# Another order of the projections, stacks and router stages within the step of an attention kernel

## The reference

```python
def attention(h, mask, ctx, Wq, Wk, Wv, Wo, gate):          # 32 heads of 16
    q, k, v = heads(h @ Wq), heads(h @ Wk), heads(h @ Wv)
    q, k = q * cos + rotate_half(q) * sin, k * cos + rotate_half(k) * sin
    own = softmax(q @ k.T / 4 + mask) @ v
    ak, av = heads(ctx @ Wk), heads(ctx @ Wv)
    return (own + tanh(gate) * softmax(q @ ak.T / 4) @ av) @ Wo

x = x + attention(layernorm(x), mask, ctx, Wq, Wk, Wv, Wo, gate)
h = layernorm(x)
value, expert = top_k(h @ router_w.T, 2)                     # of 8 experts
weight = softmax(value)
x = x + sum over the two of weight * (silu(h @ w1[expert].gate) * (h @ w1[expert].up)) @ w2[expert]
```

## Time and profile before

| | |
|---|---|
| time, median of 3 runs | 2524.99 us (2516.36 to 2528.28) |
| profiled execution | 2524.06 us |
| its span | 2522.1 us |
| TensorE, VectorE, ScalarE, GpSimd busy | 82%, 57%, 50%, 33% of the span |
| TensorE clock granted, mean | 0.914 of full speed |
| attention phase | up to about 1,950 us of the span |

### The profile page before, as it was taken

The page is one execution under the profiler, slowest core; times in us unless marked ns, Lnnn a source line. Parts: engine busy times, 40 slices in busy tenths (PEclk is TensorE's granted clock), DMA queues, the critical chain, the costliest instruction groups (busy, mean ns, idle before and its releaser), DMA issues. The chain is left out here.

```text
span 2522.1 us, 55300 instructions
## 1 busy us (share of the span) xinstructions
PE 2069.4 (82%) x18953; PEld 1234.9 (49%) x18954; DVE 1444.9 (57%) x3715; ACT 1258.6 (50%) x2260; POOL 821.0 (33%) x851
## 2 busy tenths in 40 slices
PE   4888888888788877878788888888888449999997
PEld 2455555544444444544444444544445226666664
DVE  4567666666666666666666666666666433333332
ACT  4565555555555555555455555555555234444443
POOL 2123323233233222232223232222222334444443
PEclk7899989899889888998898989899999769999999
DMA  2001111000000000010000000000001234444444
GB/s 101 21 29 32 30 35 47 29 29 29 29 29 29 29 29 29 29 29 29 29 29 29 29 29 29 29 29 29 29 25 20 52 85 83 84 83 84 83 84 66
DMA packets 69810, 105.95 MB, mean 42 GB/s; under 512 B 25024, under 2 KB 29120, under 8 KB 69120
## 3 DMA queue, kind: packets, MB, share of 16 engines
q0 software_dynamic: 24096, 37.51, 8.6%
q1 hardware_dynamic: 45536, 65.69, 8.4%
HBM read 67.51 MB, written 35.65 MB: 41 GB/s over the span
## 5 line engine op out<-in xcount | busy, mean ns | idle before, releaser
L515 ACT ACTIVATE pr<-st 128x512 f32<-128x512 f32 x512 | 305.0, 596 | 451.0 <-PE st L1083 335.1
L1051 PE MATMUL md<-kk,qz 128*128 128x128 f16 x2048 | 221.1, 248 | 203.1 <-DVE mx L714 79.9
L379 POOL TENSOR_TENSOR t<-t 128x512 f32<-128x512 f32 x64 | 81.4, 1271 | 872.1 <-DVE t L692 872.1
L710 DVE TENSOR_REDUCE mx<-md 128x4 f32<-128x512 f32 x256 | 176.5, 689 | 299.0 <-remote 218.9
L1097 PE MATMUL av<-pr,vv 128*17 128x128 f32 x4096 | 253.6, 293 | 66.4 <-issue 56.1
L1051 PEld LDWEIGHTS md<-kk,qz 128*128 128x128 f16 x2048 | 136.1, 108 | 314.3 <-issue 169.4
L1431 PE MATMUL y<-w1s,hgT 128*128 x1704 | 280.3, 315 | 4.6 <-ACT hgT L1345 4.6
L414 POOL DMA_INDIRECT lists<-row,posi x256 | 248.8, 972 | 86.4 <-issue 86.4
L1074 PE MATMUL st<-qz,kk 128*128 128x256 f16 x1024 | 204.9, 283 | 41.8 <-DVE mT L735 37.1
L507 ACT ACTIVATE qz<-ma 64x256 f16<-64x256 f16 x512 | 191.8, 375 | 79.8 <-remote 65.8
L1431 PEld LDWEIGHTS y<-w1s,hgT 128*128 128x128 f16 x1704 | 164.5, 98 | 96.6 <-issue 5.1
(11 more groups left out here) (200 smaller groups left out, 3875.0 us busy)
## 6 DMA issues: line engine op xcount, KB each, us to landing
wst<-in_w SPq DMA_DIRECT2D x32, 352.0 KB, 3.1
cin<-in_ctx SPq DMA_DIRECT2D x32, 256.0 KB, 4.1
xin<-in_x SPq DMA_DIRECT2D x32, 256.0 KB, 3.8
xres<-in_x SPq DMA_DIRECT2D x32, 256.0 KB, 3.8
out<-x SPq DMA_DIRECT2D x32, 256.0 KB, 2.1
h_pairs<-ohs SPq DMA_DIRECT2D x32, 256.0 KB
lists<-row,posi POOLq DMA_INDIRECT x256
msk<-in_mask SPq DMA_DIRECT2D x32, 64.0 KB, 3.6
```

The lines of the kernel that those rows point to most:

```text
L515: act.activation(pr[:, path, :, :], st[path][:, :, :], ACT.Exp).then_inc(p_ex.sem, 1)
L710: dve.tensor_reduce(mx[:, 1, 4 * g:4 * g + 4], sm[1][:, :, :], AX.X, ALU.max).then_inc(s_ad.sem, 1)
L1051: i = pe.matmul(sm[path][:, j, :], qz[:, h // 2, h % 2, :], keys[:, h // 2, :], start=True, stop=True)
```

## The change

TensorE's step: the query and key projections of the batch after the next now stand at the end (`q(m)` after scores 7, `k(m)` after the last turn back), so that the next step finds them done. The value projections stand between the stacks (`v` with u = 11, `avp` with u = 13) and use `ma[1]` both. Context turn, output turn, output projection, h turn and router come one or two half-groups sooner, stack 0 with u = 7 and scores 0 with u = 8. Tables at the top of the file give the places of stacks and scores and their banks. ScalarE follows. On VectorE the fourth `normal` of a batch moves from the end of its step to the start of the next, and `router_weights` and `router_rows` move from the first third of the step to behind maxima 4. GpSimd's and SyncE's lists are unchanged. `first` and `last` are adapted.

```diff
+STACK_AT = (7, 8, 9, 10, 11, 12, 14, 15)
+SCORES_AT = (8, 9, 10, 11, 12, 13, 15)
+STACK_BANK = (0, 1, 0, 1, 0, 0, 0, 1)
...
@@ scalar: own_values, stack_out
-            act.activation(vv[:, n.par, 0, :, 0:HD], heads(ma[0]), ACT.Copy, scale=1 / WS).then_inc(v_v.sem, 1)
+            act.activation(vv[:, n.par, 0, :, 0:HD], heads(ma[1]), ACT.Copy, scale=1 / WS).then_inc(v_v.sem, 1)
-            bank, pairs = half(ma[g % 2]), slice(2 * g, 2 * g + 2)
+            bank, pairs = half(ma[STACK_BANK[g]]), slice(2 * g, 2 * g + 2)
@@ scalar: step
                 exps(b, u)
-                if u == 0:
+                if u == 0 and n:
+                    ctx_hi(n)
+                    mask_hi(n)
+                if u == 1:
+                    if n:
+                        q_high(n)
                     if d:
                         out_hi(d)
+                if u == 2 and n:
+                    ctx_turned(n)
+                if u == 3 and d:
+                    out_T(d)
+                if u == 4:
                     if n:
-                        ctx_hi(n)
-                        mask_hi(n)
-                if u == 2:
-                    if n:
-                        q_high(n)
+                        k_high(n)
                     if c:
                         router_exp(c)
-                if u == 3:
-                    if d:
-                        out_T(d)
-                    if n:
-                        ctx_turned(n)
-                if u == 4 and n:
-                    k_high(n)
                 if u >= 5 and u % 4 == 1:
                     values_T(b, u // 4 - 1)
-                if u == 5:
-                    w_slice(b)
+                if u == 5 and n:
+                    ak_high(n)
                 if u == 6:
                     if d:
                         h_high(d)
-                    if n:
-                        ak_high(n)
-                if u == 8 and d:
+                    w_slice(b)
+                if u == 7 and d:
                     h_transposed(d)
                 if u == 11 and m:
                     x_high(m)
-                if u >= 8 and n:
-                    stack_out(n, u - 8)
-            values_T(b, 3)
-            if n:
-                own_values(n)
-                adapter_values(n)
+                if u == 12 and n:
+                    own_values(n)
+                if u == 14 and n:
+                    adapter_values(n)
+                if n and u in STACK_AT:
+                    stack_out(n, STACK_AT.index(u))
             if m:
                 x_turned(m)
+            values_T(b, 3)
@@ vector: neg_max, step
-            if b:
-                normal(b, 3)
             dve.wait_ge(mp_t.sem, mp_t.at(n))
             dve.tensor_copy(mT[:, :, :], m_bank()[0:3 * NH]).then_inc(m_T.sem, 1)
...
+            if n:
+                rotate_q(n)
             if d:
-                out_low(d)
+                normal(d, 3)
             if n:
                 ctx_lo(n)
                 mask_lo(n)
-                rotate_q(n)
+            if d:
+                out_low(d)
             if c:
                 router_top(c)
             if n:
                 rotate_k(n)
-            if c:
-                router_weights(c)
             if d:
                 residual(d)
                 norm_h(d, n)
-            if c:
-                router_counts(c)
-                router_rows(c)
-            if d:
                 h_low(d)
             if n:
                 ak_low(n)
+            if c:
+                router_counts(c)
             normal(b, 0)
...
             if n:
                 maxima(n, 1)
+                maxima(n, 2)
             normal(b, 1)
             if n:
-                for g in range(2, 5):
-                    maxima(n, g)
+                maxima(n, 3)
+                maxima(n, 4)
+            if c:
+                router_weights(c)
+                router_rows(c)
+            if n:
+                maxima(n, 5)
             normal(b, 2)
             if n:
-                for g in range(5, 8):
-                    maxima(n, g)
-                neg_max(n, b)
-            else:
-                normal(b, 3)
+                maxima(n, 6)
+                maxima(n, 7)
+                neg_max(n)
@@ tensor: waits of x_turn, k, v, avp, stack
-            pe.wait_ge(v_v.sem, v_v.at(n.shift(-1)))
+            pe.wait_ge(stk_o.sem, stk_o.at(n.shift(-1), GROUPS - 1))
...
-            pe.wait_ge(av_v.sem, av_v.at(n.shift(-1)))
+            pe.wait_ge(x_T.sem, x_T.at(n))
+            pe.wait_ge(stk_o.sem, stk_o.at(n.shift(-1)))
...
-            pe.wait_ge(stk_o.sem, stk_o.at(n, GROUPS - 1))
-            project(ma[0], xT, wv).then_inc(v_p.sem, 1)
+            pe.wait_ge(stk_o.sem, stk_o.at(n, 4))
+            project(ma[1], xT, wv).then_inc(v_p.sem, 1)
...
-            pe.wait_ge(stk_o.sem, stk_o.at(n))
+            pe.wait_ge(v_v.sem, v_v.at(n))
...
-            if g >= 2:
+            if g in (2, 3, 4):
                 pe.wait_ge(stk_o.sem, stk_o.at(n, g - 1))
+            if g in (5, 6):
+                pe.wait_ge(stk_o.sem, stk_o.at(n, g))
+            if g == 7:
+                pe.wait_ge(av_v.sem, av_v.at(n))
@@ tensor: step
                 if u >= 6 and u % 4 == 2:
                     values_back(b, u // 4 - 1)
+                if u == 4 and n:
+                    ak(n)
+                if u == 7 and d:
                     router(d)
+                if n and u in STACK_AT:
+                    stack(n, STACK_AT.index(u))
+                if n and u in SCORES_AT:
+                    scores(n, SCORES_AT.index(u))
                 if u:
                     values(b, u - 1)
+                if u == 1 and n:
+                    ctx_turn(n)
+                if u == 2 and d:
+                    out_turn(d)
+                if u == 3 and d:
+                    out_project(d)
                 if u == 5 and c:
                     places(c, n)
+                if u == 6 and d:
+                    h_turn(d)
+                if u == 11 and n:
+                    v(n)
+                if u == 13 and n:
+                    avp(n)
+            if m:
+                x_turn(m)
             values(b, 2 * GROUPS - 1)
             if n:
                 scores(n, GROUPS - 1)
-                v(n)
-                avp(n)
+            if m:
+                q(m)
+            if n:
+                max_turn(n)
             values_back(b, 3)
             if m:
-                x_turn(m)
-            if n:
-                max_turn(n)
+                k(m)
```

More of the change, by code:

```diff
@@ L606, in first @@
             for g in range(GROUPS):
+                if g == 5:
+                    own_values(n)
+                if g == 6:
+                    adapter_values(n)
                 stack_out(n, g)
-            own_values(n)
-            adapter_values(n)
             x_turned(n.shift(1))
@@ L714, in maxima, with neg_max @@
             dve.tensor_reduce(mx[:, 0, 4 * g:4 * g + 4], sm[0][:, :, :], AX.X, ALU.max).then_inc(s_own.sem, 1)
-        def neg_max(n, b=None):
+        def neg_max(n):
             dve.wait_ge(s_own.sem, s_own.at(n))
@@ L911, in last @@
         def last(n):
+            normal(n, 3)
             router_top(n.shift(-1))
@@ L1035, in stack @@
                 pe.wait_ge(f_cnt.sem, f_cnt.at(n.shift(-3)))
-            if g >= 2:
+            if g in (2, 3, 4):
                 pe.wait_ge(stk_o.sem, stk_o.at(n, g - 1))
-            turn_pairs(qs, ma[g % 2], 0, 2 * g, 2)
-            turn_pairs(ks, ma[g % 2], 2, 2 * g, 2)
-            turn_pairs(aks, ma[g % 2], 4, 2 * g, 2).then_inc(stk_t.sem, 1)
+            if g in (5, 6):
+                pe.wait_ge(stk_o.sem, stk_o.at(n, g))
+            if g == 7:
+                pe.wait_ge(av_v.sem, av_v.at(n))
+            bank = ma[STACK_BANK[g]]
+            turn_pairs(qs, bank, 0, 2 * g, 2)
+            turn_pairs(ks, bank, 2, 2 * g, 2)
+            turn_pairs(aks, bank, 4, 2 * g, 2).then_inc(stk_t.sem, 1)
         def scores(n, g):
@@ L1139, in step @@
                     values_back(b, u // 4 - 1)
-                if u == 9 and d:
+                if u == 4 and n:
+                    ak(n)
+                if u == 7 and d:
                     router(d)
-                if u >= 9 and n:
-                    stack(n, u - 8)
-                if u == 1 and n:
-                    q(n)
-                if u == 2 and n:
-                    k(n)
-                if u == 4 and d:
-                    out_project(d)
-                if u == 5 and n:
-                    ak(n)
+                if n and u in STACK_AT:
+                    stack(n, STACK_AT.index(u))
+                if n and u in SCORES_AT:
+                    scores(n, SCORES_AT.index(u))
                 if u:
                     values(b, u - 1)
-                if u == 3:
-                    if n:
-                        ctx_turn(n)
-                    if d:
-                        out_turn(d)
+                if u == 1 and n:
```

(19 more changed lines are left out.)

## The result

| | before | after |
|---|---|---|
| time, median (lowest to highest, 4 runs each) | 2526.64 us (2516.36 to 2531.44) | 2728.63 us (2726.52 to 2733.82) |
| profiled execution, its span | 2524.06, 2522.1 us | 2733.82, 2731.8 us |
| TensorE clock granted, mean | 0.914 | 0.883 |

The changed kernel is slower: ratio 1.081 (95% interval 1.077 to 1.085). The prediction had the sign and missed the size: 2585 was forecast, its range ended at 2655.

The account below looks back on a forecast made before the run. TensorE (82% busy) bounds front and tail, VectorE paces the middle, list DMAs lose 6.3 us. Step 56.6 + 0.4 branch + 5.0 lists + 1.0 irregular = 63.0 against 61.1; 28 steps plus 8 us give about 2585 us, range 2440 to 2655.

Parts of the forecast that it names:

- The order without lists: Whole step free of the list loss: 56.6 us against 52.2 now, plus 0.4 for the loop's backward branch.
- The lists: End of step: eight list DMAs move to x = 45.5 to 55.4, their loss onto the chain, 5.0 us (0 to 7.9).
- irregular: Whole step: 1.0 us for the pauses that already make some steps 62 to 68 us.
- Tail and front: Step's end and start: 5.2 us of projections leave the front, yet stack 0 comes at x = 25.0, now 24.0.
- high outputs to 7.2, their rests to 8.0: Front, ScalarE then VectorE: high outputs done at x = 7.2, their rests at 8.0, output projection from 10.9 to 13.5.
- the 5.2 us that left the front turn into waits of TensorE; the front gives back nothing: Front, TensorE: 5.2 us of moved projections become waits, no gain; bounds for the front minus 2 to plus 2.
- Middle: Maxima 0 at x = 27.9 to maxima 7 ending at 54.9: VectorE waits behind value projections, router operations add 2.5 us.
- rival B: Whole step: VectorE's waits close and the norm's chain comes earlier, 3 us a step less than forecast, 2495 us; chance 0.18.
- the 62.9 for a loss that stays at x = 40: Step time in us if, by the skill page's sentence, the list loss stays at x = 40 at its present cost.
- rival C: End of step: the whole list loss lies on the chain, 7.9 us instead of 5.0, total 2665 us; chance 0.15.
- The branch: Loop end: the backward branch costs 0.4 us a step, 0.8 in each second step.
- Rival A: End of step: the list loss falls off the chain behind projections needing few semaphores, step 58, total 2445 us; chance 0.22.

Follow-up runs that it names:

- outputs first: Changed kernel with high outputs ahead of high queries on ScalarE: 2669.80 us, ratio 1.046 to the kernel before.
- both cures: Changed kernel with high outputs ahead of high queries on ScalarE, and four filler matmuls before each wait of output projection, h turn and router: 2613.22 us, ratio 1.024.
- late rows: Kernel before with only router weights and rows moved behind maxima 4, so list DMAs start later: 2473.98 us, ratio 0.976.

## Why the prediction was right in sign and wrong in size

Forecast 63.0 us a step, measured 68.3; the 5.3 split as follows. The order without lists: predicted 57.0 with the branch, measured 61.0, so 4.0. The lists: predicted 5.0 plus 1.0 irregular, measured 7.4, so 1.4. The 4.0 in turn are 5.3 for lock and clock, which the sum did not have, less 1.3 that it counted too much elsewhere.

*Tail and front.* First scores at x = 2.8 (predicted 2.7), the turn's wait in the list-free step 0.73 (0.8): right. The step that failed is "high outputs to 7.2, their rests to 8.0". I gave the rests their lone duration and had read the neighbour only from the other side: the earlier trace rows show what GpSimd's rests do to a small VectorE operation, and my own order put the query rests beside the output's. It took 2.20 instead of 0.69, and output turn, projection and all behind it came 1.4 us late (projection at x = 12.3, predicted 10.9; 10.4 with outputs first). The Trainium skill's "SBUF — State Buffer", section "Who interferes with whom", says that a VectorE instruction with two SBUF inputs contends with a GpSimd instruction that reads SBUF; the trace agrees (2.20 us beside the query rests, 0.69 ahead of them), and I had used the rule at one place of the change and not at the other.

*The clock.* The second failed step: "the 5.2 us that left the front turn into waits of TensorE; the front gives back nothing". I priced the waits and not the clock behind them; in the front of the kernel before TensorE was nearly full and at 2.4 GHz. In the new one the 1.2 GHz level sets in behind waits of 1.3 to 1.8 us, also without lists, and four fillers ahead of each wait take it away: the list-free step is then 57.0. That this is almost the 56.6 that I had counted is chance, for it still holds the lock.

*Middle.* Weights and rows in their new place took 2.0 us in a piece (2.5 predicted) and met nobody: no operation among them took over 0.23, where in the kernel before (step at 1031.29) one took 1.13 and another 0.85. With lock and clock gone the list-free step has stack 0 at x = 24.4 (predicted 25.0), maxima 0 at 27.1 (27.9), the end of maxima 7 at 53.6 (54.9) and the next mT at 55.2 (56.6). So the count was sound and 1.4 too long; over all steps without lists the mean is 55.7, 1.3 under the 57.0 of the sum, and rival B was right in direction. The base was not quite one number either: list-free steps of the kernel before take 52.2 or, with the clock down once at x = 43 to 50, 54.8. Two slips changed nothing: three waits of 0.5 stand as 1.6 in the sum, and the 62.9 for a loss that stays at x = 40 leaves out branch and irregular pauses (64.3 with them).

*The lists.* That the loss travels with them, and that ScalarE stands until 7 to 9 us behind the first, held. It cost 7.4, and 8.6 with both cures, and not 5.0, close to rival C's 7.9: I had let part of it fall on waits. The same page of the Trainium skill, in its section "SBUF: two separate sides", says that a DMA can't be slowed by a compute operation, nor the other way round. For the operations the traces agree (the busy times with and without lists above); it doesn't follow that DMAs cost nothing, since the handshakes between the engines end late and the same arithmetic takes 61.1 us a step with lists and 54.0 without. What holds the handshakes back, or TensorE itself, stays open.

*The branch.* Priced at 0.4 a step, without a row to show it. In the new order mT is there before the key projection ends, so nothing covers it; it cost 2.2 us a step in the repaired order. The Trainium skill's "Runtime: NRT & Kernel Launch", section "Instruction fetch mechanics", says that a taken branch breaks the sequential prefetch. Three pairs of kernels with and without the loop fit that, with 1.8, 3.2 and 2.0 points of the time before, and so do the pauses of the kernel with late rows, which stand behind every branch and not at the loop's entry.

*Rival A* (the loss goes away behind work that waits for no one) was wrong for this kernel, where the query projection has scores 7 before it and a turn behind it. But with the lists beside the value projections of the old order the remote waits nearly vanish: that kernel is 2.4% faster than before, and 5.6% with its steps written out (part of which may be the small operations' new place).

## What to carry to other kernels

Work taken out of a full stretch of TensorE does not come back as time if a chain of other engines ends there; it turns into waits and may cost the clock as well, so fill the stretch or shorten the chain first. When steps move, look again at who meets whom: VectorE beside GpSimd, small DMAs beside handshakes, and the loop's branch beside both. Try scattered small DMAs beside the longest piece of work that waits for nobody; here it paid in one order, and why is open.

## What was not expected of the hardware

- Eight indirect DMAs of 128 rows of 8 bytes each cost 7.1 us of a 61.1 us step although nothing in it waits for their data; four cost 1.4.
- While they are on the way, the transfer of an instruction block takes 2.8 us instead of 1.0 (medians), and with late rows each of twelve backward branches held TensorE for 3.3 to 10.3 us.
- 26 steps written out instead of a loop of 13 turns were faster in all three orders tried, by 1.8 to 3.2 points.
- Sixteen matmuls a step that do no useful work, put ahead of four waits, took 3.3% off the changed kernel (ratio 1.045 against 1.081).
